# Flamingo gated cross-attention and feed-forward block: the first step on half a batch, setup work on other engines, and the drain in another order

## The reference

```python
x = x + tanh(g_xattn[0]) * xattn(layernorm(x), ctx, seg, Wq, Wkv, Wo)
x = x + tanh(g_ffn[0]) * ffn(layernorm(x), W_in, b_in, W_out, b_out)

# xattn: B=4, LQ=1024 tokens of 256, 77 context rows, 16 heads of 16
qh = split_heads(q @ Wq.T);  k, v = split(ctx @ Wkv.T)
gather = seg_id[:, :, None] - arange(4)            # four context rows of each token
scores = einsum(qh, kh[gather]) * 16 ** -0.5, masked where gather < 0
out = (softmax(scores) @ vh[gather]) @ Wo.T

# ffn: weights quantised to 8 bit by column / row, activations to 16 bit
# by the largest absolute value of the whole tensor
hidden = gelu(q16(x) @ q8(W_in) + b_in);  out = q16(hidden) @ q8(W_out) + b_out
```

## Time and profile before

| | us |
|---|---|
| median of 3 runs | 348.0 (347.28 to 349.62) |
| the profiled execution | 347.8 |
| its span | 346.0 |
| VectorE's first score product starts | 28.97 |
| VectorE's last shift of attention (step 16) ends | 195.0 |
| first matmul of `expand` | 219.3 |

### The profile page before, as it was taken

How to read it: one execution, slowest core, us unless ns; L and a number is a source line. 1 busy time by engine, 2 the same in 40 slices (tenths; PEclk the granted TensorE clock), 3 DMA queues, 4 the chain that set the end, 5 groups by cost and what they waited for, 6 DMA issues and landing times.

```text
span 346.0 us, 5842 instructions
## 1 busy us (share of the span) xinstructions
PE 286.5 (83%) x1807; PEld 213.4 (62%) x1807; DVE 306.8 (89%) x585; ACT 230.6 (67%) x425; POOL 173.5 (50%) x147
## 2 busy tenths in 40 slices
PE   3839769987879897799986557899899949999994
PEld 3417548876768785677775445344344428888883
DVE  0995887996999999999999997889999879999993
ACT  2123874687498764455464227999689969999990
POOL 1180087998789896999876940220342500110010
PEclk9985998998999998999988888899999989999999
DMA  7993000000000000000000000011112100455535
GB/s 266 283 389 119 1 1 2 0 0 3 0 1 3 0 2 0 0 2 1 3 0 0 3 1 0 2 61 61 61 64 118 62 0 2 63 68 78 97 61 121
DMA packets 6980, 17.27 MB, mean 50 GB/s; under 512 B 1318, under 2 KB 3822, under 8 KB 6446
## 3 DMA queue, kind: packets, MB, share of 16 engines
q1 hardware_dynamic: 4447, 12.31, 9.9%
q0 software_dynamic: 1008, 3.67, 7.0%
q10 hardware_dynamic: 1503, 1.02, 1.1%
HBM read 9.13 MB, written 7.86 MB: 49 GB/s over the span
## 4 chain that ended last, share of the span: by engine, by line
PE 40%; DVE 37%; ACT 9%; issue 6%; POOL 3%; DMA 3%; ACTq 0%; DVEq 0%; POOLq 0%
PE bank L826 16%; PE bank L796 12%; DVE bank L911 6%; PE bank L656 5%; DVE onehot L1015 5%; DVE prod L905 5%; PE bank L636 4%; DMA seg_i<-in_itok_BxS_dram 3%; ACT unread L465 2%; DVE hmax L1168 2%; DVE xres L959 2%; ACT unread L459 2%; DVE xmax L965 2%; DVE bn L870 1%; DVE w_i L1185 1%
## 5 line engine op out<-in xcount | busy, mean ns | idle before, releaser
L309 POOL TENSOR_TENSOR vsel<-vsel,pr 128x1024 f32<-128x1024 f32 x31 | 59.9, 1932 | 31.8 <-DVE pr L941 31.4
L636 PE MATMUL bank<-kvtab,onehot 80*128 80x256 f16 x512 | 67.0, 282 | 4.2 <-DVE prod L905 4.1
L636 PEld LDWEIGHTS bank<-kvtab,onehot 80*128 80x128 bf16 x512 | 51.5, 101 | 15.1 <-DVE prod L905 5.8
L529 ACT ACTIVATE hidden<-bank,bin__58,zscale 128x512 f32 x64 | 49.7, 777 | 7.5 <-PE bank L796 2.2
L796 PE MATMUL bank<-xhi,win 128*128 128x512 f16 x128 | 49.4, 386 | 1.9 <-DVE xlo L1163 1.9
L796 PE MATMUL bank<-xlo,win 128*128 128x512 f16 x128 | 49.3, 385 | 0.0
L905 DVE TENSOR_TENSOR prod<-bank,q 128x1024 f32<-128x1024 f32 x32 | 38.8, 1214 | 9.8 <-PE bank L636 9.7
L1228 DVE SCALAR_TENSOR_TENSOR hlo<-hq,rel_wout,hhi 128x512 f16<-128x512 int16 x64 | 45.6, 743 | 0.0
L656 PE MATMUL bank<-wqT,xT 128*128 128x256 f32 x128 | 38.1, 451 | 7.4 <-ACT xT L368 7.4
L826 PE MATMUL bank<-wout,hhi 128*128 128x256 f16 x256 | 39.1, 276 | 2.2 <-DVE hhi L1220 2.2
L312 POOL TENSOR_TENSOR vsel<-vsel 128x512 f32<-128x512 f32 x31 | 39.6, 1279 | 2.4
(11 more groups left out here) (140 smaller groups left out, 486.6 us busy)
## 6 DMA issues: line engine op xcount, KB each, us to landing
...
```

The lines of the kernel that those rows point to most:

```text
L309: pool.tensor_tensor(v3, v3, pr[k][:, t].rearrange("p o h -> p (o h)").unsqueeze(2).broadcast_to([P, KW * H, HD]), ALU.mult).then_inc(s_pv, 1)
L529: act.activation(hidden[:, g, f, :], bank, ACT.Gelu, bias=bin_[:, f:f + 1], scale=zscale[:, f:f + 1]).then_inc(s_h, 1)
L636: mm = pe.matmul(dst[:, off * D:(off + 1) * D], onehot[:, off, bass.ds(tile * P, P)], kvtab[:, b, part, col:col + D], start=(part == 0), s ...
```

## The change

What it does, by engine:

- **DMA**: batch 0 of x is loaded in two halves with a semaphore each.
- **TensorE**: projects only batch 0 ahead; W_q and W_o are transposed after x; the gather of K for tile 0 comes before W_o; batches 1, 2 and 3 are projected before pair 0's V gather, in step 2 and in step 3. In steps 2 and 3 this waits for `kv_low` of the batch before, ahead of the step's queries. `attn_out(0)` moves from the end of step 3 into step 4.
- **VectorE**: loses the copy of W_kv, the centring of W_q and the addition of epsilon (line 882). It makes the one-hots of two tiles, one K/V scale, and the first half of batch 0's statistics before its first score product; the rest comes after it. `kv_scales` is called ahead of mask and shift in steps 2 and 3. `norm_bias` comes later in a step, and the W_out maxima two steps earlier.
- **ScalarE**: gets the copy of W_kv, the centring of W_q, and the clamps of batches 1 to 3 as two Relu each (after steps 1, 2 and 3). Its statistics are called after steps 1 to 6. `norm2` comes after `evac_oT`.
- **GpSimd**: loses the clamps, gets the addition of epsilon, and handles both tiles before `inv_std2`.
- **Drain**: on ScalarE `evac_oT(15)` goes ahead of `norm2(13)`, and `round_win(0)` behind `evac_xn2T(14)`. On VectorE the residual and statistics of pair 15 go ahead of `win_levels(0)`.

```diff
 SP
-            sp.dma_start(xres[:, 0:TB, :], x_d[0]).then_inc(s_x[0], 16)
+            sp.dma_start(xres[:, 0:TB // 2, :], x_d[0, :, 0:TB // 2, :]).then_inc(s_xa, 16)
+            sp.dma_start(xres[:, TB // 2:TB, :], x_d[0, :, TB // 2:TB, :]).then_inc(s_x[0], 16)
...
 GpSimd
             def inv_std2(u, k):
 
+                pool.wait_ge(s_mv, u + 1)
+                pool.tensor_tensor(ve[k][:], mv[k][:, :, 1], consts[:, 0:2], ALU.add).then_inc(s_ve, 1)
                 pool.wait_ge(s_ve, u + 1)
...
             def step(i, k):
                 if 2 <= i < NP + 2:
                     weigh_v(i - 2, k, 0)
+                if 2 <= i < NP + 1:
+                    weigh_v(i - 2, k, 1)
                 if 4 <= i < NP + 4:
                     inv_std2(i - 4, k)
-                if 2 <= i < NP + 1:
-                    weigh_v(i - 2, k, 1)
...
 ScalarE
+            act.wait_ge(s_wkvTp, 1)
+            copy(wkvT[:].rearrange("p c e -> p (c e)"), bank45[:]).then_inc(s_wkvT, 1)
+            act.wait_ge(s_wq, 16)
+            for c in range(C):
+                ins = act.activation(unread[0][:, c, :], wq_ld[:, c, :], ACT.Copy, accum_out=wq_sum[:, c:c + 1])
...
+            def clamp_seg(b):
+
+                act.wait_ge(s_segb[b], 16)
+                v = seg_b[:, b * LQ:(b + 1) * LQ]
+                act.activation(v.rearrange("u (t p) -> u t p", t=TB), seg_i[:, b * LQ:(b + 1) * LQ].rearrange("u (p t) -> u t p", t=TB),
+                               ACT.Relu, bias=top[0:U, 0:1], scale=-1.0).then_inc(s_segr, 1)
+                act.wait_ge(s_segr, b)
+                act.activation(v, v, ACT.Relu, bias=top[0:U, 0:1], scale=-1.0).then_inc(s_segc, 1)
...
+            step(1, 1)
+            act.wait_ge(s_const, 4)
+            clamp_seg(1)
             kv_high(1)
-            evac_q(0, 0)
             act.wait_ge(s_gate, 48)
             act.activation(tanhs[:], gates[:], ACT.Tanh).then_inc(s_tanh, 1)
-            kv_high(2)
-            step(1, 1)
             stats1(1, 0)
-            kv_high(3)
             for i in range(2, NP + 1):
                 step(i, i % 2)
-                if i in (2, 4, 5, 7, 8):
-                    stats1((i + 2) // 3, 0 if i in (4, 7) else 1)
+                if i in (2, 3):
+                    kv_high(i)
+                    clamp_seg(i)
+                if 2 <= i <= 6:
+                    stats1((i + 1) // 2, (i + 1) % 2)
...
 TensorE, in step
+                if i in (2, 3):
+                    pe.wait_ge(s_kvlo, i)
+                    project_kv(i)
+                if i == 4:
+                    pe.wait_ge(s_kvlo, NB)
+                    attn_out(0, 0)
...
 VectorE, in aggregate
                 ins.then_inc(s_mv, 1)
-                dve.wait_ge(s_mv, u + 1)
-                dve.tensor_scalar(ve[k][:], mv[k][:, :, 1], LN_EPS, None, ALU.add).then_inc(s_ve, 1)
...
+            kv_low(1)
+            step(2, 0, then=lambda: kv_scales(2))
+            kv_low(2)
+            batch_onehot(1)
+            step(3, 1, then=lambda: kv_scales(3))
+            kv_low(3)
```

More of the change, by code:

```diff
@@ L745, in spread @@
                 pe.matmul(psum, ones[:], diag[:], start=True, stop=True).then_inc(done, 1)
-            step(2, 0)
-            pe.wait_ge(s_kvlo, NB)
-            for i in range(3, NP + 1):
-                if i % (TB // 2) == 1:
-                    pe.wait_ge(s_oh, i // (TB // 2) + 1)
+            pe.wait_ge(s_oh, 2)
+            for i in range(2, NP + 1):
+                if i > 2 and i % (TB // 2) == 1:
+                    pe.wait_ge(s_oh, i // (TB // 2) + 2)
                 step(i, i % 2)
@@ L971, in softmax_end, with step @@
                 probs(u, k)
-            def step(i, k, between=None):
+            def step(i, k, between=None, then=None):
                 on = lambda lag: lag <= i < NP + lag
@@ L993, in step @@
                     qk_sum(i - 1, 1 - k, 1)
+                if then is not None:
+                    then()
                 if on(5):
@@ L1069, in _ @@
             dve.wait_ge(s_neg, 1)
-            kv_scales(2, 1)
-            step(1, 1, between=lambda: kv_low(2))
-            kv_scales(3, 1)
-            step(2, 0, between=lambda: kv_low(3))
-            make_onehot(1)
+            mask(0, 0)
+            score_max(0, 0)
+            shift(0, 0)
+            kv_low(1)
[4 more added lines that the diff above has]
+            kv_low(3)
             dve.wait_ge(s_tanh, 1)
```

179 lines of the change are left out of this document (92 added, 87 removed).

## The result

The changed kernel takes 353.81 us (median of 4 runs, 352.84 to 359.62), the kernel before 347.64 beside it. The ratio is 1.016 (95% interval 1.0101 to 1.022): slower by 5.6 us. The forecast was 346.4, its range 341 to 350.5. Ratios here leave out executions in which the chip was disturbed, while medians hold all of them (the kernel before, run again with each set of experiments, had medians from 347.6 to 352.4) and the profiled executions of e5 and e12 were disturbed ones whose later marks stand late, so I compare ratios.

A forecast was written before the change was run, and what follows sets the result against it. VectorE was taken as the bound from step 9 on, TensorE and GpSimd just behind. Terms -11.7 + 8.4 - 5.8 + 1.4 + 2.6 + 3.5 = -1.6 on the profiled 347.8 gave 346.4 us, range 341 to 350.5.

The forecast's parts named there:

- new waits in steps 1 to 7: Early attention steps: VectorE's waits for exp and gathers total 11.2 us where 9.8 were, a loss of 1.4.
- the walk: Step-by-step timing from the first score product at 17.3, placing VectorE's waits for exp and gathers in the early steps.
- The price of a pair of clamps: ScalarE after steps 1 to 3: two clamps, each priced as a 1024-wide copy of 1.02, take 2.0 us.
- One-hots: VectorE's one-hot tables: 0.26 us per quarter width for batch 0; 3.3 after step 4 counted as cover for statistics.
- The start: Up to the first score product: it comes at 17.3 us instead of 28.97, a gain of 11.7.
- Epsilon, -5.8,: Attention steps: 13 epsilon operations leave VectorE, 5.6 us plus 0.2 for gaps, a gain of 5.8.
- The clock, +2.6: TensorE in steps 2 to 4: one and a half slow-clock stretches lose 2.6 us, bounds 0 to 6.5.
- The drain, +3.5: After step 16: the tail with the first W_in rounding behind the last norms makes the drain 3.5 us longer.
- The one with ScalarE as bound of steps 2 to 4 and the drain at 4.5: Steps 2 to 4 and drain: ScalarE bounds, TensorE's clock is down in all three, 351.3 us; chance 0.13.
- The GpSimd rival: Steps 9 to 16: GpSimd becomes the bound at 9.06 us a step instead of 8.7, 349.3 us; chance 0.1.
- The rival of a lead that is kept: Whole attention: TensorE stays at full clock, exp is not last, waits fall to 8, 339.4 us; chance 0.2.
- The sentence on clamps on VectorE: Early steps: three clamps on VectorE cost 2.5 us, free ScalarE of 6.1, a version 1 to 2 better.

The follow-up runs named there:

- e5: The kernel before, with only the change's new drain order on ScalarE and VectorE: ratio 1.011 to the kernel before.
- e12: The changed kernel with only the first of ScalarE's two clamp passes per batch (one-hots built from other numbers): 353.51 us, ratio 1.015.
- e1: The changed kernel with the clamps of batches 1 to 3 back on GpSimd: 347.47 us, ratio 0.998.
- e11: The changed kernel with clamps on GpSimd, the old drain order and the epsilon addition back on VectorE: 348.87 us, ratio 1.003.
- e6: The kernel before, with the epsilon addition on GpSimd and weigh_v, norm_bias and norm2 in the changed order: 350.44 us, ratio 1.007.
- e4: The changed kernel with unused matmuls filling TensorE's idle time in steps 2 to 4: 352.06 us, ratio 1.010.
- e2: The changed kernel with the old drain order on ScalarE and VectorE: 351.46 us, ratio 1.009.
- e8: The changed kernel with the clamps back on GpSimd and the old drain order: 341.64 us, ratio 0.983.
- e9: The changed kernel with the old drain order and the clamps on VectorE, one min-and-max each: 342.11 us, ratio 0.983.

## Why the prediction was wrong

The mechanism was named (exp behind clamps and statistics in steps 2, 3 and 4, the longest for pair 2), and the step that failed is the term **new waits in steps 1 to 7, +1.4**. It measured +14.2 (24.0 of waits behind the first product where 9.8 were), the slow clock included, for which the sum had 2.6 more: 4.0 forecast for the two. Of the 24.0, 11.0 are waits for exp in steps 2 to 4 (the walk had 6.2), 6.8 waits for the gathers there (2.4), and 6.2 the rest (2.6). Two things in its working were off.

- **The price of a pair of clamps: 2.0, measured 3.3.** It was taken from a 1024-wide copy from float (1.02, twice). The first pass, which reads int32 and reads it reordered, took 2.13; which of the two makes it long no run separates. e1, which takes all of it away, gives 6.3 us back. e12, with clamps of about the predicted price, lowered the waits for exp by 3.1, though not the time (1.015 against 1.016). So the wrong price is some 3 us of the waits, and the clamps as a whole, 7.0 less in e1, half of them.
- **The walk left out what the waits do to each other.** It had waits for exp of 1.5, 0.8 and 3.9; measured were 2.31, 3.39 and 5.30. One-hots for batch 1, counted at 3.3 and meant to hide the statistics of step 2, were over in 2.0, so exp was waited for instead. Time saved on VectorE ahead of a wait for ScalarE is not time saved.

**One-hots.** The sum left those of batches 1 to 3 as they had been (10.4 together) and gave batch 0 3.5. They took 2.02, 2.07 and 2.98, and 1.11 with 1.61: 4.1 to the good, which was then waited away.

**The start** was right: 17.77 against 17.3, 11.2 won instead of 11.7.

**Epsilon, -5.8,** was right in size for this setting and wrong as a sum term that stands alone. Taking it back in e11 cost 7 us; giving it to the kernel before in e6 cost 2.6. Steps that VectorE bounds pass it on (8.68 against 9.1, and e6 from step 12 on), the early ones in e6 did not. Its length of 0.43 was for the most part not its own, as e11's rows show. The sentence that `norm_bias` and `norm2` being later costs nothing is in doubt by e6.

**The clock, +2.6:** its bounds held. With no slow stretch left in steps 2 to 4, e4 was some 2 us faster, and its waits 1.8 less. I had it beside the waits; it is a part of the 14.2. The Trainium skill ("TensorE: Matmul & The Clock Gate", section HAM oscillation) would have all three stretches slow; the trace has the queries of steps 3 and 4 at 3.78 and the projection of step 2 at 3.62, but the queries of step 2 at 1.99. It was right on the pattern, and the pattern was cheap.

**The drain, +3.5:** 28.8 from step 16's end to `expand` where 28 was predicted, 24.3 before. e5 gives 3.9 for the order alone, e2 2.6 for undoing it, e1 and e8 between them 5.2. By the marks the drain took 34.6 to 36.1 in all six profiles with the new order, and 29.5 to 33.5 in the eight with the old one. The sign and nearly the size were right, and so was the reason, the tail behind `win_back(0)` (its items come to 9.2, not 9.3). So this part should not have been made.

**Step 16's end,** predicted near 190, came at 196.1: the waits were 10.2 above their forecast, clock included, and the one-hots 4.1 below.

**The rivals.** The one with ScalarE as bound of steps 2 to 4 and the drain at 4.5 (351.3) lies nearest; it had 0.13. Its waits were the right ones and still too small, 7.9 more with the clock where 14.2 were. The GpSimd rival didn't occur: 8.20 of 8.68 busy in the step shown, and the addition took 0.22 where I had guessed 0.28. The rival of a lead that is kept, 0.2, comes near e8 (339.4 against 341.6), where nothing of the clamps is ahead of exp.

The sentence on clamps on VectorE, from the rule of the Trainium skill ("ScalarE: Activation LUTs", Rules for kernel authors), said 1 to 2 us better than this change. The trace agrees with the rule itself: 1.07 us on VectorE against 2.13 and 1.15 on ScalarE. The gain was larger than I had said: e9, with the old drain, is 3.3% under the changed kernel, and e2, with that drain alone, 0.7%.

The sum by what was measured: -11.2 (start), +8.4 (work behind it), -4.1 (one-hots), -5.8 (epsilon), +14.2 (waits, clock included), +4.3 (drain) and +0.3 behind it come to +6.1, against 5.8 in the profiles. The 0.3 that is left over lies within the work terms, which I did not measure one by one.
